# Flamingo-style stack of eight blocks, last self attention: queries and keys projected for eight heads at a time, and spread in SBUF by transfers

## The reference, cut to what matters

```python
B, N, D, H, E = (4, 256, 256, 16, 8)        # here x is (2, 1024, 256)
DK = D // H                                  # 16
def _msa(x, w_qkv, w_proj):
    qkv = (x @ w_qkv).reshape(b, n, 3, H, DK)
    q, k, v = (qkv[:, :, i].transpose(0, 2, 1, 3) for i in range(3))
    attn = softmax(einsum('bhnd,bhmd->bhnm', q, k) * (1.0 / sqrt(DK)))
    y = einsum('bhnm,bhmd->bhnd', attn, v)
    return y.transpose(0, 2, 1, 3).reshape(b, n, d) @ w_proj
x = x + _msa(_layernorm(x, ln1_w, ln1_b), w_qkv, w_proj)
x = x + _moe_mlp(...)
```

## Time and profile before

| What | us |
|---|---|
| Timed runs, median of 3 (lowest to highest) | 3254.08 (3252.89 to 3259.18) |
| The profiled execution, own time | 3239.96 |
| Its span in the profile | 3238.0 |
| The block `l3a`: first instruction to the first of `l3f` | 2476.3 to 3010.9 |
| Opening: first maxima pair to first score | 2495.1 to 2519.4 |
| 16 units, 128 steps | 2519.4 to about 3000 |

### The profile page before, as it was taken

The page is one execution under the profiler, slowest core; times in us unless marked ns, Lnnn a source line. Parts: engine busy times, 40 slices in busy tenths (PEclk is TensorE's granted clock), DMA queues, the critical chain, the costliest instruction groups (busy, mean ns, idle before and its releaser), DMA issues. The chain is left out here.

```text
span 3238.0 us, 41490 instructions
## 1 busy us (share of the span) xinstructions
PE 2950.1 (91%) x16033; PEld 1580.0 (49%) x16033; DVE 1641.4 (51%) x3315; ACT 1278.0 (39%) x1784; POOL 1286.4 (40%) x1025
## 2 busy tenths in 40 slices
PE   7998899999999999697988999978887899998898
PEld 3565344444434444244467889843333223322687
DVE  4625645654554465485651222156553877675400
ACT  4433344444344444355521111124333565555232
POOL 2332466665666566701244222215555310000433
PEclk9999999999999999898999999989998999999999
DMA  1500000000000000000026556420001000000386
...
DMA packets 72758, 172.03 MB, mean 53 GB/s; under 512 B 17501, under 2 KB 52242, under 8 KB 59764
## 3 DMA queue, kind: packets, MB, share of 16 engines
...
...
## 5 line engine op out<-in xcount | busy, mean ns | idle before, releaser
L1520 POOL TENSOR_TENSOR l1x_added<-l1x_added,l1x_probs 128x1024 f32<-128x1024 f32 x224 | 527.2, 2354 | 264.5 <-ACT l1x_probs L1791 198.8
L1888 DVE TENSOR_REDUCE l1x_tops<-l1x_ring 128x1 f32<-128x512 f32 x512 | 326.6, 684 | 195.6 <-PE l1x_ring L1600 195.0
L1121 DVE TENSOR_REDUCE l3a_halves<-l3a_ring 128x1 f32<-128x512 f32 x512 | 324.7, 683 | 99.0 <-PE l3a_ring L966 94.9
L1791 ACT ACTIVATE l1x_probs<-l1x_slots 128x1024 f32<-128x1024 f32 x256 | 261.8, 1023 | 239.6 <-PE l1x_slots L1644 237.8
L1637 PE MATMUL l1x_slots<-l1x_Q,l1x_K 64*128 64x512 f32 x1152 | 310.9, 617 | 6.0 <-ACT l1x_probs L1789 4.8
L1082 ACT ACTIVATE l3a_probs<-l3a_slots 128x1024 f32<-128x1024 f32 x256 | 248.1, 1021 | 160.7 <-PE l3a_slots L986 160.7
L1659 PE MATMUL l1x_pv<-l1x_probs,l1x_V 128*64 128x512 f32 x1152 | 283.6, 608 | 0.0
L986 PE MATMUL l3a_slots<-l3a_Q,l3a_K 32*128 32x512 f32 x1024 | 150.0, 635 | 35.3 <-ACT l3a_probs L1082 34.5
L3527 DVE TENSOR_TENSOR l2f_hh<-l2f_sg,l2f_hid 128x256 f32<-128x256 f32 (+1 forms) x184 | 69.8, 380 | 217.2 <-ACT l2f_sg L3374 217.2
L3374 ACT ACTIVATE l2f_sg<-l2f_hid 128x256 f32<-128x256 f32 (+1 forms) x184 | 64.5, 351 | 280.6 <-PE l2f_hid L3290 278.3
L3290 PE MATMUL l2f_hid<-l2f_xgT,l2f_gate 128*128 128x256 f32 (+1 forms) x736 | 166.9, 349 | 2.3 <-ACT l2f_xgT L3361 1.5
...
## 6 DMA issues: line engine op xcount, KB each, us to landing
...
l2f_yg<-rows_out SPq DMA_DIRECT2D x8, 512.0 KB, 5.6
...
x<-in_x SPq DMA_DIRECT2D x4, 512.0 KB, 8.1
...
x<-x SPq DMA_DIRECT2D x4, 512.0 KB, 2.9
```

The lines of the kernel that those rows point to most:

```text
L1121: nc.vector.tensor_reduce(halves[:, k % 2, col:col + 1], bank_of(banks[e]), AX.X, ALU.max).then_inc(s["bank_done"], 1)
L1520: ins = nc.gpsimd.tensor_tensor(added[h][:], added[h][:], probs[:, n % PROBS, :, :], ALU.add)
L1791: ins = nc.scalar.activation(p, s2[m % 2], ACT.Exp)
L1888: ins = nc.vector.tensor_reduce(tops[:, e * NT + t, h:h + 1], bank, AX.X, ALU.max)
```

## The change

- `wq` and `wk` are no longer padded (256 columns). One projection yields 128 dense rows, eight heads, into `dense_q` or `dense_k`; `pair` in its event is a pair of groups. `project` and the evacuation (now a Copy without bias) run for 4 pairs and not for 8 groups.
- SyncE spreads each head: `spread_heads` issues four transfers SBUF to SBUF of 16 rows x 512 columns for each (q or k, group, half), 128 in all, with waits for the evacuation of the dense rows and for the last readers of the buffer it fills.
- The spare rows of Q and K are written once: ScalarE runs four activations of 128x1024 ahead of everything else in the block, after the load of `bqk`.
- `keep_low`, `scores` and `turn` wait for the spreading (semaphores `spread`); ScalarE waits for it before it overwrites dense rows.
- `turn` writes the shifted queries to `lifted[u % 2]`, which `scores` reads, and leaves Q as it is.
- The plan: the opening has no pieces for group 1 any more; the bfloat16 copies of group g + 1 are one burst of four; the jobs of pair p lie in steps 4, 5, 6 of unit 4p - 4 and in step 1 of the next.

```diff
+    pieces = [("v", 0, i, 1) for i in range(NT)] + [("q", 0, CH + i, 256) for i in (0, 256)]
+    for i, k in enumerate(order):
         maxima(0, [k])
-        job(*e, pool=slots)
-        if e[0] != "v" and e[2] % CH:
-            low(e[0], e[1], e[2] // CH)
+        if i < len(pieces):
+            job(*pieces[i], pool=slots)
+    low("q", 0, 1)
     turn(0)
     events.append(("begin", acts))
 
-    jobs = {}
-    for g in range(units // 2 - 1):
-        if g:
-            for i in range(2):
-                jobs[2 * g, 2 * i] = [("k", g + 1, i * CH, CH)]
-            jobs[2 * g, 4] = [("q", g + 1, 0, CH)]
-        jobs[2 * g + 1, 0] = [("q", g + 1, CH, CH)]
+    jobs, lows = {}, {}
+    for g in range(1, units // 2):
+        at = (2 * g - 2, 1) if g == 1 else (2 * g - 2, 3)
+        lows[at] = [("k", g, 0), ("k", g, 1), ("q", g, 0), ("q", g, 1)]
+    for pair in range(1, units // 4):
+        u = 4 * pair - 4
+        jobs[u, 4], jobs[u, 5] = [("k", pair, 0, CH)], [("k", pair, CH, CH)]
+        jobs[u, 6], jobs[u + 1, 1] = [("q", pair, 0, CH)], [("q", pair, CH, CH)]
     for i in range(4):
         jobs[3, 2 + i] = [("xt", 2 + i // 2, i % 2)]
         jobs[(5, 2 + 2 * i) if i < 3 else (6, i * 2)] = [("v", 1, 2 * i, 2)]
@@ -762,8 +763,8 @@
             maxima(u + 1, todo[1:2])
             for e in jobs.get((u, i), ()):
                 job(*e)
-                if e[0] in ("q", "k") and (e[2] + e[3]) % CH == 0:
-                    low(e[0], e[1], e[2] // CH)
+            for e in lows.get((u, i), ()):
+                low(*e)
             for t in outs.get((u, i), ()):
...
+        def spread_done(eng, kind, g, h):
+            eng.wait_ge(spread[kind, g % 2, h], 64 * (g // 2 + 1))
...
+            def spread_heads(kind, g, h):
+                at = slice(h * CH, (h + 1) * CH)
+                sp.wait_ge(s["job_done"], part_done(kind, g // 2, h))
+                if g >= 2:
+                    sp.wait_ge(s["low_ready"], low_at[kind, g - 2, h])
+                    if kind == "k":
+                        sp.wait_ge(s["score_psum"], NT * (2 * g - 2))
+                    else:
+                        sp.wait_ge(s["shifted"], 2 * g - 3 + h)
+                else:
+                    sp.wait_ge(s["pads_set"], 4)
+                src, to = (dense_q, Q[g % 2]) if kind == "q" else (dense_k, K[g % 2])
+                for j in range(4):
+                    row = 64 * (g % 2) + 16 * j
+                    sp.dma_start(to[32 * j:32 * j + 16, at], src[row:row + 16, at]).then_inc(spread[kind, g % 2, h], 16)
+
+            for kind, g, h in (("q", 0, 0), ("k", 0, 0), ("k", 0, 1), ("k", 1, 0), ("k", 1, 1), ("q", 1, 0), ("q", 0, 1), ("q", 1, 1)):
+                spread_heads(kind, g, h)
+            for g in range(2, U // 2):
+                for kind in ("k", "q"):
+                    for h in range(2):
+                        spread_heads(kind, g, h)
...
             def keep_low(kind, g, h):
                 src, dst = (Q, Qb) if kind == "q" else (K, Kb)
                 at = slice(h * CH, (h + 1) * CH)
-                pool.wait_ge(s["job_done"], part_done(kind, g, h))
+                spread_done(pool, kind, g, h)
                 pool.tensor_copy(dst[g % 2][:, at], src[g % 2][:, at]).then_inc(s["low_ready"], 1)
...
             def project(kind, out, g, lo, wide):
-                b, q = divmod(g, QUADS)
+                b, q = divmod(g, QUADS // 2)
...
                     pe.wait_ge(s["shifted"], u + 1)
-                    pe.wait_ge(s["job_done"], max(part_done("k", g, 0), part_done("k", g, 1)))
+                    for half in range(2):
+                        spread_done(pe, "k", g, half)
...
                 for j in range(4):
                     rows = slice(32 * j, 32 * j + 32)
-                    last = nc.tensor.matmul(slots[:, j, :], K[g % 2][rows, i * P:(i + 1) * P], Q[g % 2][rows, h * CH:(h + 1) * CH],
+                    last = nc.tensor.matmul(slots[:, j, :], K[g % 2][rows, i * P:(i + 1) * P], lifted[u % 2][rows, :],
...
-                    g, lo, wide = at
-                    q = g % QUADS
+                    pair, lo, wide = at
+                    if pair:
+                        for g in (2 * pair - 2, 2 * pair - 1):
+                            spread_done(act, kind, g, lo // CH)
                     if kind == "q":
-                        if g == 0:
-                            act.wait_ge(s["bias_ready"], 1)
-                        ins = nc.scalar.activation(Q[g % 2][:, lo:lo + wide], ps[:, 0:wide], ACT.Identity, bias=bqk[:, q:q + 1], scale=0.25)
+                        ins = nc.scalar.activation(dense_q[:, lo:lo + wide], ps[:, 0:wide], ACT.Copy, scale=0.25)
                     else:
-                        ins = nc.scalar.activation(K[g % 2][:, lo:lo + wide], ps[:, 0:wide], ACT.Identity, bias=bqk[:, 4 + q:5 + q])
+                        ins = nc.scalar.activation(dense_k[:, lo:lo + wide], ps[:, 0:wide], ACT.Copy)
                 ins.then_inc(s["job_done"], 1)
 
             def exponentials(n):
@@ -1087,6 +1117,11 @@
                     act.wait_ge(s["ot_ready"], u - 1)
                 nc.scalar.activation(raw[u % 2][:], pv[:], ACT.Copy).then_inc(s["raw_ready"], 1)
 
+            act.wait_ge(s["bias_loaded"], 16)
+            for i in range(2):
+                zeros = c.zeros[:].unsqueeze(1).broadcast_to([P, S // D, D])
+                nc.scalar.activation(Q[i][:].rearrange("p (a n) -> p a n", n=D), zeros, ACT.Copy).then_inc(s["pads_set"], 1)
+                nc.scalar.activation(K[i][:].rearrange("p (a n) -> p a n", n=D), zeros, ACT.Identity, bias=bqk[:, 4:5]).then_inc(s["pads_set"], 1)
...
 
```

More of the change, by code:

```diff
@@ L820, in self16 @@
         Q, K = [sb(f"Q{i}", [P, S]) for i in range(2)], [sb(f"K{i}", [P, S]) for i in range(2)]
+        dense_q, dense_k, lifted = sb("dense_q", [P, S]), sb("dense_k", [P, S]), [sb(f"lifted{i}", [P, CH]) for i in range(2)]
         Qb, Kb = [sb(f"Qb{i}", [P, S], BF16) for i in range(2)], [sb(f"Kb{i}", [P, S], BF16) for i in range(2)]
@@ L833, in self16 @@
         s = {n: c.semaphore(f"{name}_{n}") for n in names}
+        spread = {(kind, i, h): c.semaphore(f"{name}_{kind}_spread{i}{h}") for kind in "qk" for i in range(2) for h in range(2)}
         block = ctx.enter_context(nc.Block())
+        def spread_done(eng, kind, g, h):
+            eng.wait_ge(spread[kind, g % 2, h], 64 * (g // 2 + 1))
         def parts_of(u):
@@ L1133, in turn @@
                 dve.wait_ge(s["turned_psum"], u + 1)
-                dve.wait_ge(s["job_done"], part_done("q", g, h))
-                nc.vector.scalar_tensor_tensor(Q[g % 2][:, at], out, -1.0, Q[g % 2][:, at], ALU.mult, ALU.add).then_inc(s["shifted"], 1)
+                spread_done(dve, "q", g, h)
+                if u >= 2:
+                    dve.wait_ge(s["score_psum"], NT * (u - 1))
+                nc.vector.scalar_tensor_tensor(lifted[u % 2][:], out, -1.0, Q[g % 2][:, at], ALU.mult, ALU.add).then_inc(s["shifted"], 1)
                 dve.wait_ge(s["shifted"], u + 1)
@@ L3591, in pack16 @@
         out[0, 16] = bo
-    packed = {"q": by_partition(padded(wq)), "k": by_partition(padded(wk)), "v": by_partition(wv), "o": by_partition(out.reshape(2 * D, D)),
+    packed = {"q": by_partition(wq if dense else padded(wq)), "k": by_partition(wk if dense else padded(wk)), "v": by_partition(wv), "o": by_partition(out.reshape(2 * D, D)),
               "bqk": np.concatenate([b.reshape(4, P).T for b in bias], 1)}
@@ L3716, in lay_out @@
     w = a[n + "w_qkv"]
-    for k, v in pack16(w[:, :D], None, w[:, D:2 * D], None, w[:, 2 * D:], None, a[n + "w_proj"], None).items():
+    for k, v in pack16(w[:, :D], None, w[:, D:2 * D], None, w[:, 2 * D:], None, a[n + "w_proj"], None, dense=True).items():
         arrays["l3a_" + k] = v
```

11 lines of the change are left out of this document (3 added, 8 removed).

## The result

| | us |
|---|---|
| before, median of 12 runs | 3260.81 (3252.89 to 3264.04) |
| after, median of 12 runs | 3253.54 (3248.44 to 3258.18) |
| ratio after to before | 0.9981, 95% interval 0.9973 to 0.9990 |
| the profiled execution: own time, span | 3252.0, 3250.3 (before 3239.96, 3238.0) |

The change gains 0.19%, that is 6.2 us (3.3 to 8.8) of 3260.81; the medians lie 7.3 apart. The forecast was a gain of 7.0. The absolute forecast, 3247 us, is 6.5 us too low, though: the kernel before, at 3254.08 in its first three runs, is at 3260.81 in twelve.

What follows compares the result with a forecast made beforehand. Steps with a job end on TensorE; those without end on ScalarE, or on VectorE with three pairs. -30.4 + 17.7 + 2.8 + 2.9 = -7.0 us, off the median 3254.08 gives 3247 us, range 3241 to 3257.

Steps and rivals of the forecast that it cites:

- Jobs: -12.7: Projections in the loop's steps: 25 jobs taken out save 30.4 us, twelve put in cost 17.7 us.
- because the third pair of step 4 runs into the scores: Reason for pricing a step 5 job at 4.93 us, nearer the upper end: +1.66 over 3.27.
- Opening: +2.8: Before the loop: ScalarE's four fills and the transfers of K delay the first maxima pair by 2.8 us, ends 2.2 and +4.9.
- four transfers at 0.45 us each: In the opening, SyncE issues K's four transfers at 0.45 us each, the last at 2495.3.
- Clock: +2.9: At the emptied end of the opening TensorE's clock falls and the loop starts with it: +2.9 us, ends 0 and +5.
- The sum: -7.0: Whole kernel: -30.4 + 17.7 + 2.8 + 2.9 = -7.0 us on the profiled execution of 3239.96 us.
- off the median, 3247 us: The 7.0 us gain taken off the timed runs' median, 3254.08 us, gives a forecast of 3247 us.
- The clock holds: Rival: the loop starts at 2.4 GHz, opening costs 2.2 to 2.8; -10.2 us, 3244 us; chance 0.18.
- Transfers queue up: Rival: SyncE's transfers run one after another, delaying opening and groups; +5 us (3259) to +17 us (3271); chance 0.05.
- Edits at nothing: Edits priced at zero, including SyncE's 128 transfers: 16 of one group issued in 7.2 us, under 26.4 us of cover.
- The start costs twice: Rival: landing at 3.8 us and a lower clock for some steps more; -3 us, 3251 us; chance 0.19.
- It doesn't do what it says: Rival: steps without jobs would be no shorter, since VectorE takes over; +5.7 us, 3260 us; chance 0.03.

Runs made afterwards that it cites:

- control_before: The kernel before the change, run once more without an edit: block 534.64 us against 534.54, own time 3248.1 us.
- pads_later: Kernel after, with the four fills of spare rows on VectorE, waiting until GpSimd finished both chunks of `size`: block 523.74 us against 526.46, own time 3232.30.
- opening_kept_busy: Kernel after, plus unread TensorE projections of 256 columns in the six gaps of the opening's end: block 524.38 us against 526.46, own time 3231.88.
- pads_on_vector: Kernel after, with the four fills on VectorE behind its second chunk's statistics, not on ScalarE: block 525.47 us against 526.46, own time 3234.73.
- combined: Kernel after, with late VectorE fills, second-pair projections in the opening's gaps, later jobs spaced: block 515.97 us; ratio 0.9939 to the kernel before.

## Why the prediction was right, and where it was not

**Jobs: -12.7, measured -14.7 against before and -13.1 against its second run.** The loop without its first three steps went from 439.88 and 438.25 to 425.17. In the rows a step of two pairs without a job ends on ScalarE, as the prediction read it from unit 14, and in one of three pairs TensorE waits for VectorE ahead of the third (0.84 us in step 0 of unit 8). Each price was met: 3.50, 3.27, 3.20 without a job, 4.64, 4.91, 4.65 with one. The 1.6 us between the two runs of before are a turn at the end of unit 1 that came slower in the first of them (5.56 and 4.97 us in two steps, against 4.30 and 4.65 in control_before). The change didn't gain these. Of the choice at the earlier trace rows, "because the third pair of step 4 runs into the scores", the rows bear it out: that pair starts with the scores of step 5, and the price came behind each step of three pairs, with a job in it or without.

**Opening: +2.8, measured +4.0 for the first pair, +3.4 against the second run of before.** The term was too small in three places. The fills held up the normalisation by 2.3 us (I had 2.2), which pads_later gave back. The four transfers were issued at about 0.62 us each; the step that says "four transfers at 0.45 us each" took the price from loads out of memory (0.46 to 0.50 from one start to the next), and that costs 0.5 to 0.7 over four. And K's evacuation ended 2.8 us later, not 2.2: its projection ran for 2.70 us, where before the change it was 2.14. The granted clock was 0.50 in the 2 us from 2510; before it was 0.65 in those from 2488, and 1.00 in the next. The landing of 1.9 us lies 0.2 over the small load that I took and far below the other end, 3.8. The Trainium skill, "DMA: Bandwidth & Descriptors", section "Anatomy of one DMA — SWDGE (gpsimd) path", has about 2.0 us for transfers that GpSimd issues. SyncE issues these, and the trace comes near it, with a median of 1.9 over 64 transfers of K.

**Clock: +2.9, measured +2.3 in the first three steps and +0.2 ahead of them.** opening_kept_busy gave back 2.3 with nothing else changed, and by the other kernels it is 1.6 to 2.3. The forecast named the cause and the place, and subtracted rightly the stretch that was there before. Its parts fell out otherwise, and that the total came near is partly luck. The pairs at the lower clock, priced at +0.9, cost nothing: the last reduction ended 22.21 us behind the first pair, and 22.43 before the change. The turn and what surrounds it took 2.30 us and not 1.85. And the lower clock lasted through three steps, where I had one to two.

**The sum: -7.0, measured -8.1 in the block and -6.2 (-3.3 to -8.8) in the times.** By the terms: +4.0 + 0.2 + 2.3 - 14.7 + 0.1 = -8.1. Against control_before they are +3.4 + 0.2 + 2.2 - 13.1 - 0.9 = -8.2. So each term had its sign and its cause right. The opening was forecast 1.2 us too small, and the jobs, with 1.6 us of the first profile's own in them, made up for it.

**The step that failed is "off the median, 3247 us".** It took the median of three runs for the level of the kernel before. In twelve runs it is 6.7 us higher; off that median the same sum gives 3253.8, and 3253.54 was measured, closer than the interval of the gain (3.3 to 8.8) lets one expect. The profiled execution, 3239.96, on which the sum was made, was a second sign: it lies 13 us below the fastest of the twelve runs. The range, 3241 to 3257, held the value only because it was wide; its upper end left 3 us for a kernel whose runs spread over 11 us. The rest of the program moves in steps, in both kernels. The first load of the second block was issued at about 152 us in five of the profiles (before, pads_on_vector, opening_kept_busy, pads_later, combined) and at about 158 in the other five. Layer 2's block of experts took 508.5 us in the profile after and 495 to 497 in the others; 5.7 + 13.5 are the 19 us from above. What makes these levels wasn't tried.

**The rivals.** "The clock holds" fell by the stretches at 2536 us. "Transfers queue up" fell in the loop: even with 256 transfers the path did not wait there; in the opening it is a matter of issue, 0.6 to 0.7 us each, and not of landings one behind the other, since four land 1.9 us after the last is issued. The rule of the Trainium skill under that rival ("DMA: Bandwidth & Descriptors", "Measured (HBM→SBUF, 128 partitions, SWDGE, issued from GpSimd)"), that transfers below 64 KB are bound by descriptors, may hold, and cost nothing where the work had 26 us of cover. The price of "Edits at nothing", 16 transfers in 7.2 us, was too low (10.0 to 10.8 us measured), and it still cost nothing. "The start costs twice" had the landing at 3.8 us, which didn't come. "It doesn't do what it says" fell by the 3.50 us of step 0.
